# Queries normed head by head, softmax sums shared with VectorE, and more split tiles, in a fused decoder layer

## The chip, the cores and the metric

The kernel is written for one core of a Trainium2 chip. The metric is the device time of one execution in microseconds, taken as the median of several runs. The engines are TensorE (PE, with its weight loads PEld), VectorE (DVE), ScalarE (ACT), GpSimd (POOL) and SyncE (SP, which issues nearly all DMAs). Each works through its own queue in order and waits on semaphores.

## The reference

One decoder layer over `x` (4 batches, 256 rows, 512 features) and a context of 1601 rows per batch. Each of three parts ends in a residual and a layernorm:

```
self:   q, k, v = x Wq + bq, ...     attention over the 16 x 16 (d, e) pairs of each row
cross:  kv = [context; x]            1601 + 256 = 1857 keys
        q = rms_norm(x Wq) , k = rms_norm(kv Wk), v = kv Wv     32 heads of 128, 8 key heads
        out = softmax(q k^T / sqrt(128)) v Wo
route:  softmax over 64 logits, the 8 largest kept, out = x * sum + weights @ expert_bias
```

All is float32. The cross attention is nearly all of the work, and the change lies in it.

## The kernel before

**Units and tiles.** A unit is one batch with one key head; there are 32 (8 per batch), and v is a unit's number. Its four query heads times 256 rows make two half-units p of 512 columns, 64 in all. The 1857 keys are 15 tiles j of 128 rows (the last has 65). For each tile of each half-unit PE computes scores, keys on the partitions and queries on the 512 columns; ACT copies them out of PSUM with the key's norm as scale; DVE raises `running_max`. Eighteen steps (`WAIT`) later DVE subtracts the column maximum (`shift`, L1636), ACT takes the exponential, and two steps after that (`LAG`) PE multiplies with the values into `OT_ps`.

**Precision.** To keep fp32 accuracy with fp32r matmuls, operands are split into a high and a low part and three products are summed (`three`, L971 to L973). A probability tile can be treated in two ways. A split tile has its exponential taken twice by ACT (`P_hi` rounded, then the full one in place, L1322 and L1323), its low part by POOL (`P_lo`, L888), and three matmuls on PE. A full tile has one exponential, no low part, and one full-precision matmul (L1001, two records in the profile). `FULL` lists the full tiles j of each batch.

**Softmax sums.** POOL adds every tile of a half-unit into `acc` (L902, L906). At the end PE transposes `acc` in four pieces (job `AT`, L1134), DVE sums along the columns and takes the reciprocal, PE transposes that (job `RT`, L1140), DVE copies it to `rrow`, and two DMAs store it in memory and spread it to all partitions (`rinv_spread`). DVE then divides the output (`divide`, L1811), ACT rounds it (`OT_high`), and DVE forms its low part (`OT_low`, L1815) for the product with `Wo` (jobs `O`).

**Queries.** Two Q tiles of 128 rows with four heads each are computed per unit (jobs `Q`), copied by DVE to `natq`, and multiplied by the inverse norm of each row and head: `normalise`, one `tensor_tensor` of 128x512 per tile with the factor broadcast along 128 columns (L1675). POOL computes the factors (`newton`). PE transposes the result (jobs `QT`, L1111).

**Order.** All engines walk over the same steps s, and a table written by hand (`fill`) says which other jobs stand in a step, by c = (s + 20) mod 30. One unit is 30 steps. In the order of the table: `Q` at c = 1, 3, 7, 9; `AT` at 10 and 25; `RT` at 12 and 27; `QT` at 15 and 27; `O` at 11, 13, 21, 23; `KV` (keys and values of the next unit) at each even c. DVE drains a job one step later, before what else it has in the step; each of its steps begins with `shift` and `raise_max`. `raise_max` of step s has to be done before PE's scores of step s + 2. The factor for the queries is used at c = 13 of DVE; `QT` at c = 15 of PE waits for both tiles (`s_nat`). POOL's steps are `P_lo`, the sum, and sometimes the norms' Newton steps, a weight split (first batch only) or products of the self attention of later row tiles, which are spread over single steps (`EVENTS`).

Of the kernel before, what the change touches and what calls it, by code (L numbers as in the profile page):

```python
# [23 lines left out]
P = 128  # L24
# [21 lines left out]
def layer(nc, x_in, sWq, sbq, sWk, sbk, sWv, sbv, ctx_in, Wq, Wk, Wv, Wo, qw, kw, x1, y_out, Wr, rb, eb, final):  # L46
# [25 lines left out]
    FULL = [[2, 3, 6, 7, 10, 11, 14], [4, 5, 10, 11, 14], [6, 7, 14], [6, 7, 14]]  # L72
    FULL = [FULL[v // KVH] for v in range(UNITS)]
    HALF = [[j for j in range(NJ) if j not in FULL[v]] for v in range(UNITS)]
# [75 lines left out]
    def fill(s):  # L150
# [5 lines left out]
        if c % 2 == 0:  # L156
# [9 lines left out]
            12: [("RT", 2 * v - 3)],  # L166
# [9 lines left out]
            27: [("RT", 2 * v - 2), ("QT", v, 1)],  # L176
# [5 lines left out]
        def real(job):  # L182
            if job[0] == "X":
                return job[1] < B and job[2] < NJ
            if job[0] in ("FR", "FT", "FL", "FW", "FM"):
                return True
            return 0 <= job[1] < (HALVES if job[0] in ("RT", "O", "MT", "AT") else UNITS)
# [3 lines left out]
    def divided(s):  # L191
        return [x[1] for x in fill(s - 6) if x[0] == "RT"]
# [111 lines left out]
    def acc_no(s):  # L304
        p, j = divmod(s, NJ)
        return (NJ - 1) * p + j
# [4 lines left out]
    def left(kind, v, at):  # L311
        return NJ * (2 * v - 3) + max(kind[v - 2][at]) + 1 if kind[v - 2][at] else 0

    with ExitStack() as ctx:
# [86 lines left out]
        built = [sb(f"built{i}", [P, 2, C, P], F32R) for i in range(2)]  # L401
# [3 lines left out]
        sums = sb("sums", [P, 2, 4])  # L405
        rinv = sb("rinv", [P, 2, 4])
        rrow = sb("rrow", [4, P])
# [113 lines left out]
        s_ri = sem("row_reciprocal")  # L521
# [38 lines left out]
        def xrow_of(k):  # L560
            return row[0] if k < CTX and k % 2 else xrow[:]

# [35 lines left out]
        def _(e):  # L598
# [103 lines left out]
            def store_tile(b, n):  # L702
                k = x_no(b, n)
                src = tile[k % 3] if b == 0 else built[k % 2]
# [26 lines left out]
            def store_reciprocals(p):  # L731
                e.wait_ge(s_fr, F_AT["RT", p] + 1)
                e.dma_start(rsd[p % 2].rearrange("(i q) -> i q", q=P), rrow[:]).then_inc(s_rd, 16)
# [47 lines left out]
            for s in STEPS:  # L781
# [25 lines left out]
                for x in fill(s - 1):  # L807
                    if x[0] == "RT":
                        store_reciprocals(x[1])
                for x in fill(s - 3):  # L810
                    if x[0] == "RT":
# [30 lines left out]
        def _(e):  # L842
# [4 lines left out]
            for i in range(2):  # L847
                e.memset(f(built[i][:]), 0.0).then_inc(s_pad, 1)
                e.memset(nat[i][:], 0.0).then_inc(s_pad, 1)
            e.memset(eps[:], EPS).then_inc(s_pad, 1)  # L850
# [40 lines left out]
            def add(t):  # L891
                p, j = divmod(t, NJ)
                if j == 0:
# [4 lines left out]
                if j == 1:  # L898
                    if p >= 2:

                        e.wait_ge(s_ff, F_AT["AT", p - 2] + 1)
# [3 lines left out]
                e.wait_ge(s_acc, acc_no(t - 1))  # L905
# [60 lines left out]
        def _(e):  # L966
            e.wait_ge(s_id, 2)
            e.wait_ge(s_pad, 5)
# [919 lines left out]
```

## Time and profile before

| | us |
|---|---|
| median of 3 runs (2812.94 to 2818.02) | 2815.64 |
| the profiled execution | 2816.99 |
| its span in the profile | 2815.2 |

| engine | busy us | share of the span | instructions |
|---|---|---|---|
| PE | 2720.3 | 97% | 14812 |
| PEld | 2220.4 | 79% | 14812 |
| POOL | 2377.3 | 84% | 2320 |
| DVE | 2221.7 | 79% | 3596 |
| ACT | 2029.4 | 72% | 3945 |

A time stands for one execution; the span is from its first to its last profiled instruction. Matmuls are pipelined and their ends are modelled, so consecutive ones overlap in the records, and a price is better read from starts. Durations of DVE and POOL instructions contain the time that they wait for a port to memory.

### The profile page before, as it was taken

Reading aid. Unit: us, or ns where it says so; the run is one execution under the profiler, and the core shown is the slowest. Engines: PE = TensorE matmul, PEld = TensorE weight load, DVE = VectorE, ACT = ScalarE, POOL = GpSimd, SP = SyncE. Lnnn points to the kernel's source line nnn. Section 1 sums busy time; section 2 is a strip of 40 time slices with the busy share of each in tenths; the row PEclk is TensorE's granted clock in tenths of the full one; section 3 lists DMA queues with packets and bytes.
Section 4 is the critical chain, followed back from the end, with each engine's and each line's share of the span. In section 5 each row is a group of like instructions: output and inputs, shape, how many; then the busy total and the mean of one; then the engine's idle time right before and its main releaser. Section 6 shows DMA issues by size and latency. Waiting matters only on the chain.

```text
span 2815.2 us, 47816 instructions
## 1 busy us (share of the span) xinstructions
PE 2720.3 (97%) x14812; PEld 2220.4 (79%) x14812; DVE 2221.7 (79%) x3596; ACT 2029.4 (72%) x3945; POOL 2377.3 (84%) x2320
## 2 busy tenths in 40 slices
PE   7899999999999999999999999999999999999974
PEld 5777878777878888888888888888888888888853
DVE  5577888888778878888778887787778888788873
ACT  3577777777767777777777777777777777777771
POOL 4399999898888888878889988888898888888893
PEclk9999999999999999999999999999999999999996
DMA  6756565565555454555545455554455445344310
GB/s 234 253 184 216 193 221 193 195 213 184 183 178 200 160 177 169 182 177 196 178 147 193 167 189 174 179 184 165 156 173 173 154 158 180 124 165 150 117 42 26
DMA packets 159434, 485.64 MB, mean 173 GB/s; under 512 B 16839, under 2 KB 27849, under 8 KB 159182
## 3 DMA queue, kind: packets, MB, share of 16 engines
q1 hardware_dynamic: 157592, 481.01, 50.5%
q8 instruction: 121, 1.98, 0.3%
q10 hardware_dynamic: 1590, 1.58, 0.2%
q14 instruction: 131, 1.07, 0.1%
HBM read 403.09 MB, written 79.43 MB: 171 GB/s over the span
## 4 chain that ended last, share of the span: by engine, by line
PE 79%; POOL 9%; issue 6%; DVE 4%; ACT 2%; DMA 1%; SPq 0%; POOLq 0%; ACTq 0%; DVEq 0%
PE K_ps L971 9%; PE K_ps L973 9%; PE K_ps L972 9%; PE OT_ps L1001 7%; PE S_ps L971 6%; PE S_ps L973 6%; PE S_ps L972 6%; POOL acc L906 5%; PE OT_ps L971 5%; PE OT_ps L972 4%; PE OT_ps L973 4%; POOL P_lo L888 2%; PE F_ps L971 2%; PE F_ps L972 2%; PE F_ps L973 2%
## 5 line engine op out<-in xcount | busy, mean ns | idle before, releaser
L906 POOL TENSOR_TENSOR acc<-acc,scores 128x512 f32<-128x512 f32 (+1 forms) x832 | 1120.8, 1347 | 40.4 <-ACT scores L1323 10.1
L888 POOL TENSOR_TENSOR P_lo<-scores,P_hi 128x512 fp32r<-128x512 f32 x672 | 898.4, 1337 | 211.3 <-ACT scores L1323 210.3
L1652 DVE SCALAR_TENSOR_TENSOR running_max<-S_ps,rk,running_max 128x512 f32<-128x512 f32 (+1 forms) x896 | 669.0, 747 | 250.2 <-ACT scores L1309 247.8
L1636 DVE TENSOR_TENSOR scores<-scores,Mb_ps 128x512 f32<-128x512 f32 (+1 forms) x960 | 648.7, 676 | 134.4 <-PE Mb_ps L1127 134.3
L1309 ACT ACTIVATE scores<-S_ps,rk 128x512 f32<-128x512 f32 (+1 forms) x960 | 651.6, 679 | 139.8 <-PE S_ps L973 120.1
L1323 ACT ACTIVATE scores<-scores 128x512 f32<-128x512 f32 (+1 forms) x960 | 596.9, 622 | 59.2 <-DVE scores L1636 57.1
L1322 ACT ACTIVATE P_hi<-scores 128x512 fp32r<-128x512 f32 x672 | 423.1, 630 | 293.7 <-DVE scores L1636 213.9
L971 PE MATMUL S_ps<-QT_hi,KT_hi 128*128 128x512 f32 (+1 forms) x960 | 496.9, 518 | 14.8 <-DVE running_max L1652 13.0
L971 PE MATMUL K_ps<-Wkv_hi,kvT 128*128 128x256 f32 (+1 forms) x1664 | 470.9, 283 | 2.4 <-DVE kvT L1709 2.4
L973 PE MATMUL K_ps<-Wkv_hi,kvT 128*128 128x256 f32 (+1 forms) x1664 | 471.1, 283 | 0.0
L972 PE MATMUL K_ps<-Wkv_lo,kvT 128*128 128x256 f32 (+1 forms) x1664 | 470.3, 283 | 0.0
L973 PE MATMUL S_ps<-QT_hi,KT_lo 128*128 128x512 f32 (+1 forms) x960 | 380.6, 396 | 0.0
L972 PE MATMUL S_ps<-QT_lo,KT_hi 128*128 128x512 f32 (+1 forms) x960 | 379.3, 395 | 0.0
L971 PEld LDWEIGHTS K_ps<-Wkv_hi,kvT 128*128 128x128 f32 (+1 forms) x1664 | 310.3, 186 | 22.4 <-DVE kvT L1709 2.8
L972 PEld LDWEIGHTS K_ps<-Wkv_lo,kvT 128*128 128x128 f32 (+1 forms) x1664 | 310.3, 186 | 20.1
L971 PE MATMUL OT_ps<-P_hi,V_hi 128*128 128x512 f32 x672 | 290.3, 432 | 31.0 <-POOL P_lo L888 30.8
L973 PEld LDWEIGHTS K_ps<-Wkv_hi,kvT 128*128 128x128 f32 (+1 forms) x1664 | 310.7, 187 | 0.0
L1001 PE MATMUL OT_ps<-scores,V_full 128*128 128x512 f32 (+1 forms) x576 | 296.7, 597 | 0.0
L971 PEld LDWEIGHTS S_ps<-QT_hi,KT_hi 128*128 128x128 f32 (+1 forms) x960 | 178.1, 186 | 119.3 <-DVE running_max L1652 46.5
L972 PE MATMUL OT_ps<-P_lo,V_hi 128*128 128x512 f32 x672 | 266.6, 397 | 0.0
L973 PE MATMUL OT_ps<-P_hi,V_lo 128*128 128x512 f32 x672 | 266.0, 396 | 0.0
L972 PEld LDWEIGHTS S_ps<-QT_lo,KT_hi 128*128 128x128 f32 (+1 forms) x960 | 178.9, 186 | 92.4 <-issue 64.1
(226 smaller groups left out, 4666.8 us busy)
## 6 DMA issues: line engine op xcount, KB each, us to landing
kvT<-kvT_scratch SPq DMA_DIRECT2D x403, 512.0 KB, 3.7
Wq_hi<-weight_halves_scratch SPq DMA_DIRECT2D x48, 512.0 KB, 5.4
Wq_lo<-weight_halves_scratch SPq DMA_DIRECT2D x48, 512.0 KB, 6.6
Wo_hi<-weight_halves_scratch SPq DMA_DIRECT2D x48, 512.0 KB, 4.7
Wo_lo<-weight_halves_scratch SPq DMA_DIRECT2D x48, 512.0 KB, 5.6
kvT_scratch<-built SPq DMA_DIRECT2D x45, 512.0 KB, 4.3
rinv_spread<-rinv_scratch SPq DMA_DIRECT2D x64, 256.0 KB, 4.8
Wkv_hi<-weight_halves_scratch SPq DMA_DIRECT2D x24, 512.0 KB, 5.6
```

What stands on the lines that cost most here:

```text
L888: e.tensor_tensor(P_lo[n % PB][0:r, :], prob(t)[0:r, :], f(P_hi[n % PB][0:r, :]), ALU.subtract)\
L906: e.tensor_tensor(a[0:r, :], a[0:r, :], prob(t)[0:r, :], ALU.add).then_inc(s_acc, 1)
L971: e.matmul(out, l_hi, r_hi, start=first, stop=False)
L972: e.matmul(out, l_hi, r_lo, start=False, stop=False)
L973: return e.matmul(out, l_lo, r_hi, start=False, stop=last)
L1001: ins = e.matmul(OT_ps[:], V_full[v % 2][0:r, FULL[v].index(j), :], row[t % RING][0:r, :], start=first, stop=last)
L1309: e.activation(row[s % RING][0:r, :], S_ps[s % 2][0:r, :], ACT.Copy, scale=rk[0:r, v % 2, j:j + 1])\
L1322: e.activation(P_hi[n % PB][0:r, :], d, ACT.Exp)
L1323: e.activation(d, d, ACT.Exp).then_inc(s_p, 1)
L1636: e.tensor_tensor(d, d, Mb_ps[0:r, :], ALU.add).then_inc(s_d, 1)
L1652: e.scalar_tensor_tensor(a, src, k, a, ALU.mult, ALU.max).then_inc(s_top, 1)
```

## The change

Five things, all in the cross attention:

- `normalise` is called for one Q tile at a time, tile 0 at c = 13 and tile 1 at c = 14 of DVE, and does four `tensor_scalar` of 128x128 per tile, one for each head, with the factor as a per-partition scalar.
- Tiles 2, 7 and 11 of each half-unit are no longer added into `acc`. DVE sums each of them in blocks of 32x32 (`tensor_reduce` with `apply_transpose`, 128x512 to 128x16), one step after its shift. In the last unit (`LATE`) all 15 tiles go this way and nothing is added on POOL. At the end DVE reduces `acc` in the same way and adds up the blocks (`sum_blocks`, at c = 9 and 24).
- Job `AT` is now one product of 16x32 on PE, `sums` times a 0/1 matrix `same`, which gives the row sums in the layout of `rrow`; DVE takes the reciprocal straight into `rrow`. The four transposes of `acc`, the job `RT`, its copy and its reciprocal go.
- The store and the spread of the reciprocals follow `AT` and so come two steps earlier; `divide`, `OT_high` and `OT_low` come one step earlier.
- The lists of full tiles shrink from 7, 5, 3, 3 to 5, 3, 1, 1 tiles for the four batches. The products of the later self attention go to the steps of tiles 2, 7, 11 (`LIGHT`). `built` has one buffer in place of two.

```diff
-    FULL = [[2, 3, 6, 7, 10, 11, 14], [4, 5, 10, 11, 14], [6, 7, 14], [6, 7, 14]]
+    FULL = [[0, 1, 12, 13, 14], [12, 13, 14], [14], [14]]
+    SUMMED = [[2, 7, 11]] * B
+    LIGHT = [[2, 7, 11]] * B
+    SUMMED = [SUMMED[v // KVH] for v in range(UNITS - 1)] + [list(range(NJ))]
...
-            12: [("RT", 2 * v - 3)],
...
-            27: [("RT", 2 * v - 2), ("QT", v, 1)],
+            27: [("QT", v, 1)],
...
     def divided(s):
-        return [x[1] for x in fill(s - 6) if x[0] == "RT"]
+        return [x[1] for x in fill(s - 7) if x[0] == "AT"]
...
-        if j in FULL[p // 2] and j - 1 not in FULL[p // 2] and j < NJ - 1:
+        if j in LIGHT[p // 2]:
             EVENTS.append(s)
...
+            def add_blocks(p):
+                e.wait_ge(s_bt, p + 1)
                 out = take(("AT", p))
-                for i in range(4):
-                    ins = e.transpose(out[:, i * P:(i + 1) * P], acc[p % 2][:, i * P:(i + 1) * P], ident[:])
+                e.matmul(out[0:16, 0:32], sums[:, p % 2, :], same[:], start=True, stop=True).then_inc(s_ff, 1)
...
-            def normalise(v):
+            def normalise(v, t):
                 e.wait_ge(s_nw, 5 * RT_AT["q", v] + 5)
-                e.wait_ge(s_kr, K_AT["Q", v, 1] + 1)
-                for t in range(TPB):
-                    factor = rq[:, 4 * t:4 * t + 4].unsqueeze(2).to_broadcast([P, GR, HD])
-                    e.tensor_tensor(natq[t][:], natq[t][:], factor, ALU.mult).then_inc(s_nat, 1)
+                e.wait_ge(s_kr, K_AT["Q", v, t] + 1)
+                for h in range(GR):
+                    ins = e.tensor_scalar(natq[t][:, h, :], natq[t][:, h, :], rq[:, 4 * t + h:4 * t + h + 1], None, ALU.mult)
+                ins.then_inc(s_nat, 1)
...
-                    e.reduce_sum(sums[:, p % 2, :], out.rearrange("p (i k) -> p i k", k=P), AX.X).then_inc(s_fr, 1)
-                    e.reciprocal(rinv[:, p % 2, :], sums[:, p % 2, :]).then_inc(s_ri, 1)
+                    e.reciprocal(rrow[:], out[0:16, 0:32]).then_inc(s_fr, 1)
...
+            def sum_tile(t):
+                p, j = divmod(t, NJ)
+                e.wait_ge(s_p, t + 1)
+                e.tensor_reduce(blocks_of(p)[:, SUMMED[p // 2].index(j), :], prob(t).rearrange("p (j a) -> p j a", a=32), AX.X,
+                                ALU.add, apply_transpose=True).then_inc(s_bs, 1)
...
-                for kind, v in rooted(s - 4):
-                    if kind == "q":
-                        normalise(v)
+                for t in range(TPB):
+                    for kind, v in rooted(s - 4 - t):
+                        if kind == "q":
+                            normalise(v, t)
+                if 0 <= s - WAIT - 1 < NS and summed_tile(s - WAIT - 1):
+                    sum_tile(s - WAIT - 1)
+                for x in fill(s + 1):
+                    if x[0] == "AT":
+                        sum_blocks(x[1])
```

## Rows read from the trace of the kernel before

**Rows 1.** The page, busy time of each engine.
```profile
PE 2720.3 (97%) x14812; PEld 2220.4 (79%) x14812; DVE 2221.7 (79%) x3596; ACT 2029.4 (72%) x3945; POOL 2377.3 (84%) x2320
```

**Rows 2.** Stages: stretch, its us, busy PE, PEld, DVE, ACT, POOL, clock, DMA.
```profile
88.80:748.80 660.00, 646.24 (x3509) 522.25 (x3510) 524.71 (x846) 488.60 (x927) 576.39 (x543) 0.99 0.60 206
748.80:2062.80 1314.00, 1309.51 (x7295) 1087.68 (x7294) 1059.78 (x1690) 994.98 (x1946) 1148.36 (x1141) 1.00 0.52 176
2062.80:2651.00 588.20, 582.90 (x3252) 485.74 (x3251) 492.05 (x813) 439.27 (x868) 509.26 (x507) 1.00 0.46 152
...
2720.00:2815.20 95.20, 50.71 (x148) 30.44 (x146) 40.96 (x79) 23.66 (x45) 47.94 (x38) 0.71 0.10 34
```

**Rows 3.** Timeline of PE: start us, us, what it is.
```profile
1508.06 1.02 PE L1001 MATMUL OT_ps<-scores,V_full 65*128 65x512 f32 x2
...
1509.16 0.39 PE L972 MATMUL S_ps<-QT_lo,KT_hi 128*128 128x512 f32 x1
1509.39 0.40 PE L973 MATMUL S_ps<-QT_hi,KT_lo 128*128 128x512 f32 x1
1509.63 0.60 PE L1134 MATMUL F_ps<-ident,acc 128*128 128x128 f32 x4
1510.06 0.60 PE L1102 MATMUL F_ps<-ident,nat 128*128 128x128 f32 x4
```

**Rows 4.** Groups by line: count, busy us, mean ns, idle before.
```profile
L906 POOL TENSOR_TENSOR acc<-acc,scores 128x512 f32<-128x512 f32 x768 | 1038.4, 1352 | 31.2 <-ACT scores L1323 10.1 <-POOL acc L906 0.4
L888 POOL TENSOR_TENSOR P_lo<-scores,P_hi 128x512 fp32r<-128x512 f32 x672 | 898.4, 1337 | 211.3 <-ACT scores L1323 210.3
...
L1660 DVE TENSOR_REDUCE ss_k<-sq 128x4 f32<-128x512 f32 x96 | 65.3, 680 | 30.1 <-ACT sq L1419 29.9
...
L945 POOL TENSOR_TENSOR Wq_lo<-w_stage,Wq_hi 128x1024 fp32r<-128x1024 f32 x16 | 38.6, 2414 | 8.8 <-ACT Wq_hi L1449 8.8
```

**Rows 5.** DMA issues: what, count, KB, median us to landing.
```profile
kvT_scratch<-built SPq DMA_DIRECT2D x45, 512.0 KB, 4.3
```

**Rows 6.** Instructions of three lines: least, median, most ns.
```profile
L1675 DVE TENSOR_TENSOR natq<-natq,rq x64: 669/1764/2155, 83.7 to 2633.0; 128x512 f32<-128x512 f32 x64
...
L1776 DVE TENSOR_SCALAR w_stage<-w_stage,self_small x12: 534/547/1652, 2194.6 to 2661.3; 128x512 f32<-128x512 f32 x12
...
L1768 DVE TENSOR_SCALAR self_small<-self_small x8: 170/686/891, 2189.6 to 2809.7; 128x2 f32<-128x2 f32 x8
```

**Rows 7.** Timeline of DVE at a normalisation.
```profile
1802.63 3.34 DVE L1675 TENSOR_TENSOR natq<-natq,rq 128x512 f32<-128x512 f32 x2
1805.89 0.68 DVE L1636 TENSOR_TENSOR scores<-scores,Mb_ps 128x512 f32<-128x512 f32 x1
1806.49 0.74 DVE L1652 SCALAR_TENSOR_TENSOR running_max<-S_ps,rk,running_max 128x512 f32<-128x512 f32 x1
```

**Rows 8.** Timeline of POOL at the same place.
```profile
1802.43 1.29 POOL L888 TENSOR_TENSOR P_lo<-scores,P_hi 128x512 fp32r<-128x512 f32 x1
1803.68 1.74 POOL L906 TENSOR_TENSOR acc<-acc,scores 128x512 f32<-128x512 f32 x1
1805.38 1.75 POOL L888 TENSOR_TENSOR P_lo<-scores,P_hi 128x512 fp32r<-128x512 f32 x1
```

**Rows 9.** Timeline of ACT at the same place.
```profile
1803.46 0.62 ACT L1323 ACTIVATE scores<-scores 128x512 f32<-128x512 f32 x1
```

**Rows 10.** Timeline of PE at the same place.
```profile
1808.26 0.40 PE L971 MATMUL S_ps<-QT_hi,KT_hi 128*128 128x512 f32 x1
...
1808.95 0.60 PE L1111 MATMUL F_ps<-ident,natq 128*128 128x128 f32 x4
```

**Rows 11.** Timeline of POOL and DVE in the last half-unit.
```profile
2737.64 1.27 POOL L902 TENSOR_TENSOR acc<-scores 128x512 f32<-128x512 f32 x1
...
2765.83 2.68 POOL L906 TENSOR_TENSOR acc<-acc,scores 128x512 f32<-128x512 f32 x2
...
2780.74 0.69 DVE L1811 TENSOR_TENSOR OT_n<-OT_n,rinv_spread 128x512 f32<-128x512 f32 x1 [5.61 <-DMA rinv_spread<-rinv_scratch]
```

More of the change, by code:

```diff
@@ L312, in left @@
         return NJ * (2 * v - 3) + max(kind[v - 2][at]) + 1 if kind[v - 2][at] else 0
+    BLOCKS = []
+    for s in STEPS:
+        if 0 <= s - WAIT - 1 < NS and summed_tile(s - WAIT - 1):
+            BLOCKS.append(s - WAIT - 1)
+        BLOCKS += [("acc", x[1]) for x in fill(s + 1) if x[0] == "AT" and x[1] not in LATE]
+    BLOCK_AT = {x: n for n, x in enumerate(BLOCKS)}
     with ExitStack() as ctx:
@@ L400, in layer @@
         xrow = sb("xrow", [P, E])
-        built = [sb(f"built{i}", [P, 2, C, P], F32R) for i in range(2)]
+        built = sb("built", [P, 2, C, P], F32R)
         ident = sb("ident", [P, P])
@@ L404, in layer @@
         nm = sb("nm", [P, 2, 4])
-        sums = sb("sums", [P, 2, 4])
-        rinv = sb("rinv", [P, 2, 4])
-        rrow = sb("rrow", [4, P])
+        blocks = sb("block_sums", [P, 2, max(map(len, SUMMED[:-1])) + 1, 16])
+        sums = sb("block_totals", [P, 2, 16])
+        same = sb("same_in_block", [P, 32])
+        rrow = sb("rrow", [16, 32])
         rb_all = sb("rinv_spread", [P, QW])
@@ L703, in store_tile @@
                 k = x_no(b, n)
-                src = tile[k % 3] if b == 0 else built[k % 2]
+                src = tile[k % 3] if b == 0 else built
                 e.wait_ge(s_fr, F_AT["X", b, n] + 1)
@@ L847, in _ @@
             for i in range(2):
[L848 removed]
                 e.memset(nat[i][:], 0.0).then_inc(s_pad, 1)
+            e.memset(f(built[:]), 0.0).then_inc(s_pad, 1)
             e.memset(eps[:], EPS).then_inc(s_pad, 1)
@@ L892, in add @@
                 p, j = divmod(t, NJ)
-                if j == 0:
+                if t not in ADD_AT:
                     return
@@ L1307, in copy_scores @@
                         e.wait_ge(s_pv, t + 1)
-                    e.wait_ge(s_acc, acc_no(t + 1 if t % NJ == 0 else t))
+                    if summed_tile(t):
+                        e.wait_ge(s_bs, BLOCK_AT[t] + 1)
+                    else:
+                        e.wait_ge(s_acc, ADD_AT[t + 1 if t % NJ == 0 else t] + 1)
+                if r < P and p in LATE:
+                    e.activation(row[s % RING][TAIL // 32 * 32:P, :], row[s % RING][TAIL // 32 * 32:P, :], ACT.Copy,
+                                 scale=0.0).then_inc(s_z, 1)
+                    e.wait_ge(s_z, LATE.index(p) + 1)
                 e.activation(row[s % RING][0:r, :], S_ps[s % 2][0:r, :], ACT.Copy, scale=rk[0:r, v % 2, j:j + 1])\
@@ L1706, in drain @@
                         k = x_no(b, n)
-                        to = tile[k % 3] if b == 0 else built[k % 2]
+                        to = tile[k % 3] if b == 0 else built
                         hi, dst = to[:, 0, :, 0:r], to[:, 1, :, 0:r]
```

81 lines of the change are left out of this document (49 added, 32 removed).

## The prediction

> **What bounds the kernel now.** I read the busy shares first: TensorE is busy 97% of the span [rows 1]. Then the stages: between 749 and 2063 us PE is busy 1309.5 of 1314 us, at full clock, while DVE, ACT and GpSimd (POOL) each have room [rows 2]. In the first batch PE idles 13.8 of 660 us, and only after 2720 us is it really idle, 44.5 of 95 us [rows 2]. So for some 2560 us the order of work on PE sets the time, and another engine counts only when it makes PE wait. After 2720 us it is the other way round: POOL runs a low part and a sum for each tile without a pause, and PE has time to spare [rows 11].
>
> A busy PE is not PE at its peak, so PE prices are taken from starts. A 512-column fp32r matmul starts 0.23 us after the one before (1509.16 to 1509.39). A full-precision PV tile takes from 1508.06 to 1508.93, 0.87 us (the next score's second matmul, at 1509.16, is 0.23 behind its first). A split tile is three times 0.23, 0.69 us [rows 3].
>
> **What PE gets back.** Each half-unit drops four transposes of `acc`, 0.43 us (1509.63 to 1510.06 [rows 3]), and one transpose of the reciprocals, a quarter of that, 0.11. It adds one product with 32 columns. No row has one; a 512-column full tile is two passes of 0.43, so 32 columns are at least 2 x 0.03 us; two passes at the price of a 128-column transpose are at most 0.22; I take 0.1, nearer to the narrow end. 0.44 us x 62 half-units = 27 us (the last two belong to the tail).
> The four batches' lists of full tiles hold 7, 5, 3 and 3 tiles before and 5, 3, 1 and 1 after, each for 16 half-units: 288 become 160, and 128 tiles become split, four in each unit. 124 of them lie outside the tail: x 0.18 us = 22 us. PE's saving is 49 us (bounds 42 to 53) if nobody else becomes late.
>
> **What the others do.** POOL loses the sums of tiles 2, 7 and 11 in 62 half-units and all 28 of the last two, 214 x 1.35 = 288 us, and gains 128 low parts x 1.34 = 171 us [rows 4]: 117 us less. DVE gains 216 block sums and 62 reductions of `acc`. The nearest row is a plain 128x512 reduction, 0.68 us [rows 4]; the transposed form has none. It reads the same columns, so I put nothing below that; above I allow twice, 1.36; I take 0.68, the row's. 278 x 0.68 = 189 us, less 64 x 0.68 = 44 for the reduction of the transposed sums that goes; the small reciprocals, copies and totals about cancel. DVE has 254 us idle between 749 and 2063 us alone [rows 2], and nothing waits on a block sum within its step: 0, or +25 us if it costs double and meets two drains in a step. The total of an `acc` is needed by PE one step later: 0, or 0.3 us x 62 = 19 where the scores' drains come first. ACT gets 128 more exponentials of 0.62 us [rows 9] and 32 copies; it idles 319 of those 1314 us [rows 2]: 0. The single `built` buffer needs its store landed (4.3 us [rows 5]) before the next build, six steps of 2.7 us later at the closest: 0. The division and its low part move one step earlier, and the DMAs of the reciprocals two; the spread has four steps to land where it had three: 0. In the first batch POOL's weight splits (2.4 us [rows 4]) now fall on steps that also have a low part (tiles 3, 7, 11), so POOL runs behind there by about 1.2 us a unit: 0 to 10 us, and 0 where PE is late anyway for the next reason.
>
> **The normalisation of the queries.** This is where I expect the loss. Before, DVE does two instructions of 128x512. The least of the 64 is 0.67 us, the median 1.76 [rows 6]: most of it is waiting, and the timeline shows for what. The pair starts at 1802.63 [rows 7] under POOL's low part of 1802.43, which ends at 1803.72; the second of the pair sits under POOL's sum of 1803.68, which itself lasts 1.74 instead of 1.29 us, because it let the first DVE instruction pass [rows 8]. The two engines take turns, whole instruction by whole instruction: 3.34 us for 1.3 us of work. Of the 32 pairs, for which this one stands, 29 have a second instruction of over 1.5 us: POOL got in between.
> The change makes eight instructions of 128x128 of the two, four in each of two steps, single-source with a scalar. Do these take turns too? A 128x512 one takes 0.53 us alone and up to 1.65, and one of 128x2 takes 0.17 alone and 0.69 in the median [rows 6]. So size doesn't protect: the price is per instruction, 0.26 us each (between 0.17 for 2 columns and 0.54 for 512), plus the rest of a POOL instruction whenever POOL has one ready.
> The Trainium skill has a rule for this: the GPSIMD Engine Reference (8. Key points) says that POOL shares its SBUF interfaces with VectorE and contends with DVE instructions in a two-port mode or with two SBUF inputs, and VectorE: DVE Perf Modes (The perf-mode tier table) gives fp32 `tensor_scalar` from SBUF the doubled rate that uses both ports. By that rule the new form is quicker alone and no freer of POOL than the old; the trace agrees, by the 0.69 us of the two-column instruction.
>
> Now the steps, by the clock of rows 7 to 10. At 1802.5 POOL has four instructions to hand: low part and sum of one tile, and of the next, whose exponential ends at 1804.08 [rows 9]. None is saved by the change (the tiles there are 4 and 5, and 6 in the step after). POOL instructions are 1.25 us apart, about 1.35 with a short DVE one let through; they end at 1803.7, 1805.05, 1806.4 and 1807.75, and one DVE instruction goes after each. The first four are done at 1808.0, where the whole pair had been done at 1805.97. The next shift and maximum take 0.6 and 0.75, to 1809.35; PE's next scores, planned for 1808.26 [rows 10], come 1.1 us late. The drain of the output goes on to 1809.9. Tile 6's exponentials, begun when its shift ends at 1808.7, end at 1809.85, so POOL again has two instructions ready: the second four end at 1809.9 + 2 x 1.3 + 0.7 = 1813.2. The transposes of the queries, planned for 1808.95 [rows 10], wait for the eighth: **4.3 us late**, the 1.1 included. Before, the pair had ended 3 us ahead of them. DVE and POOL catch up while PE stands still, so I see no second stall behind it.
> That is 4.3 us in each of 31 units, times 29/32 for the share of pairs in which POOL came between: 121 us. Bounds: if POOL never gets in between, the first four take 1.2 + 4 x 0.26 = 2.3 us, the second four no more, and all end before 1808.95: 0. If in the first batch a weight split of 2.4 us lies ahead of the first instruction, 1 us more in 7 units: 128.
>
> **The tail.** In the last half POOL's tiles take from 2737.64 to 2768.51, 30.9 us for 15, at two instructions each [rows 11]. Without the sums one is left; POOL (1.3 us), DVE (shift and block sum, 2 x 0.6 by starts) and ACT (two exponentials of 0.6) are then about level: 15 x 1.3 = 19.5 us, 11 less. In the half before, PE still has scores, and I take 8. Between the last sum and the division at 2780.74 [rows 11] lie four transposes, a reduction and a second transposition beside the two DMAs; a small reduction and a product take their place, for which I take 3 us off. 22 us in all (bounds 8 and 30).
>
> **Sum.** PE idles 23.6 us between 89 and 2651 us [rows 2]; a third of that should fall into the new waits, -8. So -27 - 22 - 22 + 121 - 8 = +42 on the profiled execution's 2816.99 us (span 2815.2), 2859 us. That execution was 1.35 above the median 2815.64; against the median 2858.
>
> **Rivals.**
> - A, not slower: POOL doesn't get in between the four short instructions, or once only. For it: in 3 of 32 pairs it didn't, and four in a row offer themselves within 1 us. Against: the other 29, and a short instruction holds the port for less of its time than a long one, which leaves POOL more room. It decides below two POOL instructions per four. 2816.99 - 71 = 2746, against the median 2745; with POOL behind in the first batch up to 2755.
> - B: POOL comes between about half the time. The first four end near 1806, the second near 1810.5, 1.5 us late: 47 - 71 = -24, against the median 2792 us.
> - C: the transposed reduction costs double. 25 us on top of the forecast, 2883.
> - D: the tail doesn't give its 22 us, since DVE with its block sums becomes what it waits for: 2880.
>
> **Chances.** The forecast's case, C and D in it, 0.60 (2825 to 2890 alone); A 0.28; B 0.12. A measurement here can tell 0.2% (5.6 us) from no change. Slower: the 0.60 and 0.01 of B; within: 0.04 of B; faster: A and the other 0.07, 0.35. The range 2742 to 2890 holds A, B and nearly all of the forecast's case.
>
> **What would show it.** Right: the DVE timeline at the normalisation has groups of four short instructions that last about 5 us, with a POOL instruction between each; the query transposes follow a PE gap of some 4 us per unit that is put down to `natq`; PE's idle time between 749 and 2063 us grows from 4.5 to some 60. PE's own saving is right if its busy time falls by about 45 us all the same; POOL's by about 117; the tail's if the last half's tiles come 1.3 us apart. Wrong: short instructions with a median near 0.26 us, a PE as full as now and a time near 2746; or a transposed reduction far over 0.68 us.

## The result, and the profile after

The changed kernel takes 2958.11 us (median of 4 runs, 2953.44 to 2963.43) against 2816.83 for the kernel before beside it: ratio 1.0502, 95% interval 1.0484 to 1.052, **141 us slower**. The forecast was 42 us slower, 2858, in a range of 2742 to 2890. Its direction came out, and so did the mechanism of its largest term; its sum was 99 us short.

The page of the kernel after, busy times (span 2961.6 us), against [rows 1]:

```profile
PE 2758.3 (93%) x14748; PEld 2253.4 (76%) x14748; DVE 2524.2 (85%) x4003; ACT 2088.7 (71%) x4107; POOL 2245.0 (76%) x2233
```

POOL lost 132 us (forecast 117) and DVE gained 302. The stages, columns as in [rows 2], from the first scores on; the last is the tail:

```profile
93.30:780.00 686.70, 642.64 (x3399) 518.39 (x3400) 588.05 (x907) 484.79 (x933) 536.42 (x512) 0.96 0.57 191
780.00:2180.00 1400.00, 1338.40 (x7303) 1113.44 (x7302) 1218.18 (x1898) 1030.32 (x2038) 1105.64 (x1115) 0.98 0.50 168
2180.00:2816.80 636.80, 604.77 (x3296) 501.23 (x3295) 558.55 (x913) 462.28 (x924) 493.18 (x503) 0.97 0.43 142
2885.20:2961.60 76.40, 42.69 (x142) 27.02 (x142) 49.17 (x98) 26.68 (x51) 23.59 (x18) 0.77 0.13 42
```

PE idled 4.5 of 1314 us before [rows 2]; now it idles 61.6 of 1400 ("some 60" was the sign given). Two other signs did not show: PE's busy time should have fallen by 45 us and rose by 38, since many matmuls now run at half clock (in e1 below, without the short instructions, it falls by 16); and the low parts of the last half come 1.5 us apart (14 in 21.0 us), not 1.3. The waits of PE name the reason (us in total, times, the longest):

```profile
PE F_ps L1132 <- DVE natq L1699: 75.6, 31, 2.7
PE S_ps L992 <- DVE running_max L1677: 49.4, 53, 3.1
PE OT_ps L992 <- POOL P_lo L909: 18.5, 28, 1.8
PE F_ps L1139 <- DVE running_max L1677: 12.4, 17, 3.2
```

One wait in each unit but the first: the transposes of the queries wait for the last normed tile. The groups behind it, against [rows 4, 6]:

```profile
L1699 DVE TENSOR_SCALAR natq<-natq,rq 128x128 f32<-128x128 f32 x256 | 250.8, 1038 | 1.0 <-POOL rq L951 0.3
L1831 DVE TRANSPOSE_TENSOR_REDUCE block_sums<-scores 128x16 f32<-128x512 f32 x186 | 128.9, 693 | 0.0
...
L1841 DVE TRANSPOSE_TENSOR_REDUCE block_sums<-acc 128x16 f32<-128x512 f32 x62 | 43.5, 702 | 0.5 <-POOL acc L927 0.4
```

A normalising instruction of 128 columns takes 1038 ns in the mean, and 270 at least; the transposed reduction costs 0.69 us, as taken (so not rival C).

**Read one unit closely.** DVE of the kernel after in unit 21 (start us, us, what), to lay beside [rows 7]:

```profile
1912.70 0.75 DVE L1677 SCALAR_TENSOR_TENSOR running_max<-S_ps,rk,running_max 128x512 f32<-128x512 f32 x1 [0.39 <-ACT scores L1330]
1913.44 5.05 DVE L1699 TENSOR_SCALAR natq<-natq,rq 128x128 f32<-128x128 f32 x4
1918.41 0.67 DVE L1661 TENSOR_TENSOR scores<-scores,Mb_ps 128x512 f32<-128x512 f32 x1
1919.01 0.74 DVE L1677 SCALAR_TENSOR_TENSOR running_max<-S_ps,rk,running_max 128x512 f32<-128x512 f32 x1
1919.67 0.67 DVE L1773 TENSOR_TENSOR y<-y,F_ps 128x512 f32<-128x512 f32 x1
1920.26 2.90 DVE L1699 TENSOR_SCALAR natq<-natq,rq 128x128 f32<-128x128 f32 x4
```

POOL at the same place:

```profile
1913.36 1.29 POOL L909 TENSOR_TENSOR P_lo<-scores,P_hi 128x512 fp32r<-128x512 f32 x1
1914.61 1.30 POOL L927 TENSOR_TENSOR acc<-acc,scores 128x512 f32<-128x512 f32 x1
1915.85 1.31 POOL L909 TENSOR_TENSOR P_lo<-scores,P_hi 128x512 fp32r<-128x512 f32 x1
1917.10 1.30 POOL L927 TENSOR_TENSOR acc<-acc,scores 128x512 f32<-128x512 f32 x1
1920.34 1.32 POOL L909 TENSOR_TENSOR P_lo<-scores,P_hi 128x512 fp32r<-128x512 f32 x1 [1.94 <-ACT scores L1344]
1921.62 1.26 POOL L927 TENSOR_TENSOR acc<-acc,scores 128x512 f32<-128x512 f32 x1
```

Count: the first four short instructions last 5.05 us beside four POOL instructions, each short one until a POOL instruction ends; the second four last 2.90 beside two (their own durations are 0.27, 1.29, 1.30 and 0.27 us). Without POOL four last 0.86 (unit 0). PE there:

```profile
1919.80 0.50 PE L992 MATMUL S_ps<-QT_hi,KT_hi 128*128 128x512 f32 x1 [0.55 <-DVE running_max L1677]
...
1923.22 0.93 PE L1132 MATMUL F_ps<-ident,natq 128*128 128x128 f32 x4 [2.47 <-DVE natq L1699]
1923.80 0.78 PE L992 MATMUL OT_ps<-P_hi,V_hi 128*128 128x512 f32 x1
1924.37 0.63 PE L993 MATMUL OT_ps<-P_lo,V_hi 128*128 128x512 f32 x1
1924.80 0.63 PE L994 MATMUL OT_ps<-P_hi,V_lo 128*128 128x512 f32 x1
```

PE waits 0.55 and 2.47 us, and then its 512-column matmuls start 0.43 us apart (1924.37 to 1924.80), not 0.23 [rows 3]. The windows say why (columns as in [rows 2]; the granted clock is the value behind POOL's):

```profile
1920.00:1923.20 3.20, 0.75 (x3) 0.28 (x2) 3.20 (x6) 1.90 (x5) 2.54 (x2) 1.00 0.97 338
1923.20:1926.60 3.40, 3.38 (x11) 2.81 (x12) 3.40 (x7) 2.81 (x6) 1.29 (x1) 0.54 0.34 134
```

After 3.2 us with PE busy for 0.75, 3.4 us are granted 0.54, about the lower level (1.2 GHz). Between the first and the last scores the trace has 33 such stretches at half clock, 157 us in all, at least one in nearly every unit; the kernel before has 3 there, 10 us.

### The profile page after: what moved, and what is told of

Same layout as the page of the kernel before. It is cut to its first block, busy times and chain, and to the rows that moved or that the text cites. A ratio compares the mean times of both kernels' runs of the same rounds, so it can differ in the third digit from the quotient of the medians.

```text
span 2961.6 us, 48211 instructions
## 1 busy us (share of the span) xinstructions
PE 2758.3 (93%) x14748; PEld 2253.4 (76%) x14748; DVE 2524.2 (85%) x4003; ACT 2088.7 (71%) x4107; POOL 2245.0 (76%) x2233
## 4 chain that ended last, share of the span: by engine, by line
PE 56%; POOL 15%; DVE 13%; issue 12%; ACT 2%; DMA 1%; POOLq 0%; ACTq 0%; SPq 0%; DVEq 0%
DVE natq L1699 7%; PE K_ps L992 6%; PE K_ps L993 6%; PE K_ps L994 6%; POOL acc L927 6%; POOL P_lo L909 5%; PE S_ps L992 5%; PE S_ps L994 4%; PE S_ps L993 4%; PE OT_ps L992 4%; PE OT_ps L994 4%; PE OT_ps L993 4%; PE OT_ps L1022 3%; DVE running_max L1677 2%; DVE scores L1661 1%
## 5 line engine op out<-in xcount | busy, mean ns | idle before, releaser
L909 POOL TENSOR_TENSOR P_lo<-scores,P_hi 128x512 fp32r<-128x512 f32 x800 | 1055.1, 1320 | 451.3 <-ACT scores L1344 450.6
L1343 ACT ACTIVATE P_hi<-scores 128x512 fp32r<-128x512 f32 x800 | 504.1, 630 | 499.2 <-DVE scores L1661 348.8
L927 POOL TENSOR_TENSOR acc<-acc,scores 128x512 f32<-128x512 f32 x620 | 829.3, 1338 | 33.0 <-ACT scores L1344 23.2
L992 PE MATMUL S_ps<-QT_hi,KT_hi 128*128 128x512 f32 (+1 forms) x960 | 448.7, 467 | 52.0 <-DVE running_max L1677 49.4
L992 PE MATMUL K_ps<-Wkv_hi,kvT 128*128 128x256 f32 (+1 forms) x1664 | 478.5, 288 | 2.4 <-DVE kvT L1734 2.4
L994 PE MATMUL K_ps<-Wkv_hi,kvT 128*128 128x256 f32 (+1 forms) x1664 | 475.9, 286 | 0.0
L992 PE MATMUL OT_ps<-P_hi,V_hi 128*128 128x512 f32 x800 | 351.0, 439 | 19.1 <-POOL P_lo L909 18.5
L992 PEld LDWEIGHTS K_ps<-Wkv_hi,kvT 128*128 128x128 f32 (+1 forms) x1664 | 319.5, 192 | 24.1 <-DVE kvT L1734 2.9
L993 PE MATMUL OT_ps<-P_lo,V_hi 128*128 128x512 f32 x800 | 321.4, 402 | 0.0
L994 PE MATMUL OT_ps<-P_hi,V_lo 128*128 128x512 f32 x800 | 320.8, 401 | 0.0
L994 PEld LDWEIGHTS K_ps<-Wkv_hi,kvT 128*128 128x128 f32 (+1 forms) x1664 | 317.9, 191 | 0.0
L1699 DVE TENSOR_SCALAR natq<-natq,rq 128x128 f32<-128x128 f32 x256 | 250.8, 1038 | 1.0 <-POOL rq L951 0.3
```

What stands on the lines that cost most here:

```text
L909: e.tensor_tensor(P_lo[n % PB][0:r, :], prob(t)[0:r, :], f(P_hi[n % PB][0:r, :]), ALU.subtract)\
L927: e.tensor_tensor(a[0:r, :], a[0:r, :], prob(t)[0:r, :], ALU.add).then_inc(s_acc, 1)
L992: e.matmul(out, l_hi, r_hi, start=first, stop=False)
L993: e.matmul(out, l_hi, r_lo, start=False, stop=False)
L994: return e.matmul(out, l_lo, r_hi, start=False, stop=last)
L1343: e.activation(P_hi[n % PB][0:r, :], d, ACT.Exp)
```

## The experiments

Times are medians; ratios are against the kernel before, run beside them. Its median was 2815.5 to 2818.9 us on the different occasions, so a difference between two of these times is good to about 3 us. "Unit" is one head's cycle of 30 score tiles, measured between first score matmuls; c is the step in it. Each experiment has a name (e1, e2, ...) that is used later.

**1. Take the change apart.** e1 is the changed kernel with the normalisation of before (both tiles in one step):

```diff
-            def normalise(v, t):
+            def normalise(v):
...
-                for h in range(GR):
-                    ins = e.tensor_scalar(natq[t][:, h, :], natq[t][:, h, :], rq[:, 4 * t + h:4 * t + h + 1], None, ALU.mult)
-                ins.then_inc(s_nat, 1)
...
+                for t in range(TPB):
+                    factor = rq[:, 4 * t:4 * t + 4].unsqueeze(2).to_broadcast([P, GR, HD])
+                    e.tensor_tensor(natq[t][:], natq[t][:], factor, ALU.mult).then_inc(s_nat, 1)
```

> The changed kernel with only the normalisation of before (two 128x512 instructions at c = 13). Theory 1 (turn-taking of the eight short DVE instructions with POOL, and what PE loses after the stall): all of the loss is gone and the saving of the rest shows, 2816.8 - 71 = 2746, between 2738 and 2765. Rival (DVE is overloaded by the block sums, the normalisation only adds to it): over 2850.

e1 measured 2833.16, ratio 1.0059 (1.0044 to 1.0074), which neither theory had. So the normalisation costs 125 us in the changed kernel, near the 121 of the forecast, and all the rest costs 16 us where a saving of 71 had been forecast: 87 us are missing there. e2 is the kernel before with only the new normalisation:

> The kernel before with only the new normalisation (eight 128x128 instructions, four each at c = 13 and 14). Theory 1: the trace of the changed kernel shows units 5.4 us longer than their PE work in the middle batches and 7 to 9 in the others, so 31 x 5.4 to 31 x 7: 2816.8 + 167 to 217, 2985 to 3030; about 5 us a unit at least, over 2960. Rival (overload by the block sums): 2816.8 + 31 x 1 to 2, 2850 to 2880.

e2 measured 2899.58, ratio 1.0298 (1.0279 to 1.0316), between the two theories: alone the normalisation costs 83. It costs 42 more beside the other parts of the change, so the parts don't simply add up.

**2. The clock.** e5: 22 transposes whose result nobody reads, on PE, ahead of the wait for the normed queries.

> The changed kernel with 22 transposes of the identity (0.11 us each, 2.4 us, results overwritten) put on PE just before it waits for the normed queries, as long as its gap there (2.47 us). Theory of the clock: PE's clock falls to half for 3.4 us after each such gap, 1.7 us lost a unit; with PE busy through the wait the clock stays up: 31 x 1.7 = 53 us less, 2905. Rival (what is lost beyond the gap is DVE and POOL catching up): no change, 2950 to 2970.

2946.43, ratio 1.0454 (1.0436 to 1.0472). The mean granted clock of the profiled executions rises from 0.966 to 0.985, as high as in e1, but the time falls by 12 us only (53 was the theory): the wait is DVE's and stays. By units: 17 to 22 fall from 85.3 to 84.2 us, 23 to 30 from 88.9 to 87.4, but units 1 to 14 gain nothing. There PE gets steps c = 15 and 16 faster and then waits longer in the steps behind. So the half clock costs some 1.1 to 1.5 us a unit where DVE and POOL have no other backlog, and is hidden behind their backlog elsewhere.

**3. The normalisation on ACT** (e6), eight `activation(..., scale=rq)`, out of POOL's way:

> The changed kernel with the eight 128x128 normalisations on ACT (activation with the factor as scale) instead of DVE. Theory 1: ACT shares no port with POOL, so each lasts about 0.3 us as its 128x128 instruction in the trace (0.31), no waiting: as fast as the old form or a little faster, since DVE is free of 3.2 us a unit: 2735 to 2750. Rival: ACT is late with its exponentials at c = 13 and 14, 1 us each: over 2770.

2834.57, ratio 1.0074 (1.0051 to 1.0098), the same as the old form on DVE and not the 2735 to 2750 of theory 1. The 256 short ones last 387 to 423 ns on ACT, beside the same POOL, and PE waits for them once. So eight short instructions cost nothing on an engine that doesn't take turns with POOL; what was still missing lay elsewhere.

**4. Where the other 87 us are.** All start from e1 (2833 us). The lines that differ from e1 (for e8 to e10 only the new one is shown):

```diff
 e7  -        return [x[1] for x in fill(s - 7) if x[0] == "AT"]
     +        return [x[1] for x in fill(s - 8) if x[0] == "AT"]
 e8  +    SUMMED = [[]] * B
 e9  +    FULL = [[2, 3, 6, 7, 10, 11, 14], [4, 5, 10, 11, 14], [6, 7, 14], [6, 7, 14]]
 e10 +    LIGHT = [[2, 6, 10]] * B
```

> After with the normalisation of before (2833 us), and the division and the low parts that follow it put back into the steps of before (steps 18 and 3 of the cycle, not 17 and 2). The first version's whole loss against its expectation (about 88 us) is unexplained. Theory 1, VectorE's step 17 is overfull (in units 1 to 7 it took 3.8 us there against 2.1 before, then ScalarE's and TensorE's steps 18 wait): about 20 us come back, 2808 to 2818. Rival, the place of the division does not matter, only the work added to VectorE does: 2828 to 2838.

e7: 2834.08, ratio 1.0061 (1.0046 to 1.0076): the division's place costs nothing here; theory 1 fell.

> After with the normalisation of before (2833 us), and GpSimd adding the tiles 2, 7 and 11 of each half again, except in the last unit: only the accumulated tile is reduced by blocks. Theory 1, VectorE's block sums (six a unit of 0.69 us, 129 us in all) delay the score copies' readers while it is the fuller engine: 2785 to 2805. Rival, GpSimd was the late engine in the first batch, and what VectorE took from it was paid back: 2830 to 2850.

e8: 2891.14, ratio 1.0267 (1.0251 to 1.0283), **58 us slower** than e1, the opposite of theory 1 and more than the rival's: the block sums are the best part of the change. Units 1 to 7 take 92.0 us each instead of 87.5.

> After with the normalisation of before (2833 us), and the list of unsplit tiles of before. The prediction priced the 124 more split tiles at 22 us of TensorE: by that 2855. Rival, the further splits cost on the other engines (low parts on GpSimd, high parts on ScalarE) what they save on TensorE in the first half of the run: 2825 to 2840.

e9: 2804.75, ratio 0.9954 (0.9939 to 0.997), **28 us faster** than e1, more than the rival's 8 at most: with the old list of unsplit tiles it beats the kernel before by half a per cent. The further splits lose where they should have gained 22. By units: unit 0 +4.2 us for the changed list, units 1 to 7 +2.8 each, 8 to 14 +0.5, but 17 to 22 -0.35. Look at unit 4 of e1, DVE and then POOL:

```profile
504.55 0.70 DVE L1831 TRANSPOSE_TENSOR_REDUCE block_sums<-scores 128x16 f32<-128x512 f32 x1
505.17 2.69 DVE L1622 TENSOR_TENSOR self_x<-self_x,self_small 128x512 f32<-128x512 f32 x1
507.79 0.67 DVE L1661 TENSOR_TENSOR scores<-scores,Mb_ps 128x512 f32<-128x512 f32 x1
```

```profile
503.67 1.32 POOL L909 TENSOR_TENSOR P_lo<-scores,P_hi 128x512 fp32r<-128x512 f32 x1
504.92 2.39 POOL L966 TENSOR_TENSOR Wo_lo<-w_stage,Wo_hi 128x1024 fp32r<-128x1024 f32 x1
507.26 1.74 POOL L909 TENSOR_TENSOR P_lo<-scores,P_hi 128x512 fp32r<-128x512 f32 x1
```

POOL had no gap since tiles 10 and 11 became split: its weight split starts late and sits in front of the two-source `self_x`, which waits to its end. The next scores come 2.9 us late. With the old list POOL had idled 2.0 us before that weight split and PE waits 0.6 there. In units 1 to 6 PE waits 16.3 us for `running_max` against 5.1.

> After with the normalisation of before (2833 us), and the later self-attention products issued beside tiles 2, 6 and 10 (the places of the first batch before) in place of 2, 7 and 11; all else as there. With 2, 7 and 11 their VectorE sums, three steps on, fall into steps 17 and 2, where the moved division stands too; with 2, 6 and 10 they fall into 16 and 1. Theory 1 (that meeting makes step 17 late): 2808 to 2820. Rival: 2828 to 2838.

e10: 2852.17, ratio 1.0125 (1.0104 to 1.0146), 19 slower than e1: theory 1 fell again, and the rival missed too. Beside 6 and 10 POOL now has a low part and a sum; beside 7 and 11 DVE had taken the sum. That suggests that the number of instructions that POOL has in one step counts; e14 and e19 below put this to the test, with mixed success.

**5. The same parts with the old list of unsplit tiles.** e11 has the new normalisation:

> The changed kernel with nothing but the list of unsplit tiles put back. The same edit took 28 us off the version with the old normalisation (2833 to 2805). The new normalisation cost 125 us in the changed kernel and 83 us in the kernel before. Theory 1, the extra 42 us come from GpSimd, which the splits made late in the first batches: here it costs 83, 2883 to 2895. Rival, they come from VectorE's block sums, which leave it no time to catch up after the eight short instructions: 2920 to 2935.

2880.31, ratio 1.0219 (1.0193 to 1.0244): against e9 the normalisation costs 76, although the block sums are there, so the extra comes from the splits. The trace shows it directly; DVE, POOL and PE in unit 21, to lay beside the fences above:

```profile
1852.93 5.05 DVE L1699 TENSOR_SCALAR natq<-natq,rq 128x128 f32<-128x128 f32 x4
...
1859.75 1.53 DVE L1699 TENSOR_SCALAR natq<-natq,rq 128x128 f32<-128x128 f32 x4
```

```profile
1859.32 1.29 POOL L927 TENSOR_TENSOR acc<-acc,scores 128x512 f32<-128x512 f32 x1 [1.42 <-ACT scores L1344]
```

```profile
1861.34 0.66 PE L1132 MATMUL F_ps<-ident,natq 128*128 128x128 f32 x4 [1.07 <-DVE natq L1699]
```

Tile 6 is unsplit, POOL has one instruction there and not two, the second four last 1.53 us and not 2.90, PE waits 1.07 and not 2.47, and no half-clock stretch follows. In units 10 to 16, where tiles 4 and 5 are unsplit, the first four last 2.93. So the splits make the wait 1.4 us longer, and behind the longer wait comes the half clock.

> The version with the old normalisation and the old list of unsplit tiles (2805 us), with GpSimd adding tiles 2, 7 and 11 again outside the last unit: before's division of labour, save for the reduction of the accumulated tile, the tail and the places of the self-attention products. With the longer list of splits this edit cost 58 us. Theory 1, GpSimd is late only where it has the splits' low parts as well: 2795 to 2808 here. Rival, it is late in the first batch in either case, because products now meet additions at 7 and 11: 2815 to 2840.

e15: 2825.44, ratio 1.0027 (1.0017 to 1.0037), in the rival's range: here the block sums give 21 us (58 with the splits).

> The version with the old normalisation, the old list of unsplit tiles and no block sums outside the last unit (2825 us), with the later self-attention products beside the tiles of before (2, 6, 10 in batch 0; 4, 10 in batch 1; 6 in the others). It differs from the kernel before by the block reduction of the accumulated tile with its one product, the division one step earlier, the single buffer for built tiles, and the last unit. Theory 1, three products a half in batch 1 beside split tiles cost there (units 8 to 14 took 84.7 us each against 83.0): 2800 to 2812. Rival, the places are worth nothing outside the split list: 2820 to 2828.

e18: 2814.23, ratio 0.9992 (0.9983 to 1.0002), between the two theories: the places of the products were worth 11 us, most of it in batch 0 (units 1 to 7 fall from 85.2 to 84.4 us) and not in batch 1, where theory 1 had put it (84.7 to 84.3). The rest of the change (block reduction of `acc` and one product, earlier division, one buffer, last unit) is no gain that can be told from none.

> The version with the old normalisation and the old list of unsplit tiles (2805 us), with the last unit handled as all others: GpSimd adds all its tiles but 2, 7 and 11, VectorE reduces the sum at the end. The prediction gave the tail 22 us: by that 2824 to 2829. Rival D of the prediction, that the tail gives nothing: 2803 to 2808.

e13: 2809.76, ratio 0.9975 (0.9965 to 0.9985), against 2804.75 in e9: putting all sums of the last unit on DVE gives 5 us net. It takes 8.4 off the stretch from the last scores to the end (85.8 to 77.4), and costs 5.0 in unit 31 itself (63.6 to 68.6).

> The version with the old normalisation and the old list of unsplit tiles (2805 us), with VectorE's block sums put on tiles for which GpSimd also has a low part (4, 8, 12 in batch 0; 2, 7, 12 in batch 1; none in batches 2 and 3), and the self-attention products beside tiles 2, 6 and 10, which have no low part in batch 0. Theory 1, what counts is GpSimd's load step by step: 2788 to 2800. Rival, VectorE's load counts and the places are worth nothing: 2803 to 2812.

e14: 2811.58, ratio 0.998 (0.997 to 0.9989), 7 slower than e9 and in the rival's range. Batch 0 got faster (83.8 us a unit against 84.7), batches 1 and 3 slower (84.6 against 83.7, and 85.3 against 84.8 in units 25 to 30). So theory 1 held in batch 0 alone. Since sums and products moved together, the run doesn't say which of them slowed batch 1.

**6. The normalisation's price, from both sides.** e3: the short instructions joined, the two steps kept:

```diff
-                for h in range(GR):
-                    ins = e.tensor_scalar(natq[t][:, h, :], natq[t][:, h, :], rq[:, 4 * t + h:4 * t + h + 1], None, ALU.mult)
-                ins.then_inc(s_nat, 1)
+                factor = rq[:, 4 * t:4 * t + 4].unsqueeze(2).to_broadcast([P, GR, HD])
+                e.tensor_tensor(natq[t][:], natq[t][:], factor, ALU.mult).then_inc(s_nat, 1)
```

> The changed kernel with each of the two normalising steps doing its tile by one broadcast multiplication over 512 columns (as before the change) in place of four of 128; steps, waits and all else as in the changed kernel (2958 us). Theory 1, the price lies in the eight short instructions taking turns with GpSimd (5.05 and 2.90 us for the two tiles in units 15 to 31): two of about 1.8 us leave the second tile at most 1.1 us shorter but the first 3.2 us, the wait at step 15 goes, and 2840 to 2865. Rival, the price lies in giving the second tile its own later step: 2900 to 2930.

2832.62, ratio 1.0055 (1.0036 to 1.0075), the time of e1: the later step costs nothing, **cutting each multiplication in four costs all 125 us**. The edit changes the kind of instruction too, but alone the two kinds differ little (0.86 us for four of 128 columns, 0.68 for one of 512). The other side, e17: eight short ones with unsplit tiles around them,

```diff
-    FULL = [[0, 1, 12, 13, 14], [12, 13, 14], [14], [14]]
+    FULL = [[2, 3, 4, 5, 6, 7, 14], [4, 5, 6, 7, 14], [4, 5, 6, 7, 14], [4, 5, 6, 7, 14]]
```

> The changed kernel with the unsplit tiles put where the queries are normalised (2 to 7 and 14 in batch 0, 4 to 7 and 14 in the other batches), so that GpSimd has one operation a step there, not two. That is two more unsplit tiles in each half of batches 2 and 3 than before the change, about 0.16 us each. Theory 1, how long the eight short instructions take is set by what GpSimd has queued beside them: in the version with the old list they took 2.93 us for the first tile where tiles 4 and 5 were unsplit and 1.53 for the second where 6 and 7 were; here they take both, and the normalisation's cost falls from 76 us there (2880) to under 20: 2820 to 2850. Rival, the splits slow the changed kernel through GpSimd's total, not at this place: 2875 to 2895.

2821.26, ratio 1.0018 (1.0008 to 1.0028), as theory 1 had it, **137 us under the changed kernel** by one list. Its DVE and POOL:

```profile
1737.21 2.93 DVE L1699 TENSOR_SCALAR natq<-natq,rq 128x128 f32<-128x128 f32 x4 [0.39 <-POOL rq L951]
...
1741.92 1.52 DVE L1699 TENSOR_SCALAR natq<-natq,rq 128x128 f32<-128x128 f32 x4
```

```profile
1737.13 2.73 POOL L927 TENSOR_TENSOR acc<-acc,scores 128x512 f32<-128x512 f32 x2
1741.48 1.28 POOL L927 TENSOR_TENSOR acc<-acc,scores 128x512 f32<-128x512 f32 x1 [1.62 <-ACT scores L1344]
```

The missing corner, e21, has the same list with the old form:

> The changed kernel with the normalisation of before and the unsplit tiles at 2 to 7 and 14 in batch 0, 4 to 7 and 14 in the others: the partner of the kernel with the new normalisation and this list (2821 us). Theory 1, the short instructions cost little where GpSimd has one operation a step beside them: 2805 to 2815, that is 6 to 16 us for the normalisation against 125 with the changed list. Rival, this list is simply faster for all, the normalisation costs 75 still: about 2746.

2804.38, ratio 0.9949 (0.9934 to 0.9964): the normalisation costs 17 us there (19 by the ratios). The four pairs:

| unsplit tiles | old form | new form | price |
|---|---|---|---|
| 4 to 7 (and 2, 3) | 2804.4 (e21) | 2821.3 (e17) | 17 |
| as before, changed kernel | 2804.8 (e9) | 2880.3 (e11) | 76 |
| as before, kernel before | 2816.8 | 2899.6 (e2) | 83 |
| as changed | 2833.2 (e1) | 2958.1 | 125 |

**7. Use it.** e19: old list, block sums on split tiles in batch 0 and the products on its unsplit ones (only the new lines):

```diff
+    SUMMED = [[4, 8, 12], [2, 7, 12], [2, 7, 11], [2, 7, 11]]
+    LIGHT = [[2, 6, 10], [4, 10], [6], [6]]
```

> The version with the old normalisation and the old list of unsplit tiles (2805 us), with block sums on 4, 8, 12 in batch 0, on 2, 7, 12 in batch 1, on 2, 7, 11 in batches 2 and 3, and the later self-attention products where they were before the change. Theory 1, GpSimd's load step by step sets batches 0 and 1 and VectorE's does not: 2788 to 2799. Rival: 2802 to 2812.

2801.14, ratio 0.9947 (0.9932 to 0.9962), 4 us under e9 and between the two theories. Then e20: batch 1's sums back on 2, 7, 11 and, from unit 16 on, one multiplication a tile in two steps:

> The combination (2801 us) with block sums on 2, 7, 11 in batch 1 too, and the normalisation as one broadcast multiplication a tile, in two steps from unit 16 on. Theory 1: units 17 to 30 get about 0.3 us each (as the one-operation form against the old one in the changed kernel, 80.24 against 80.58 us a unit), batch 1 about 0.2 each: 2793 to 2799. Rival, what is left in these units is TensorE's own work: 2800 to 2804.

**2791.77, ratio 0.991 (0.9893 to 0.9926)**, faster than both kernels. The reason given holds in part: units 8 to 14 gained 0.6 us each and 23 to 30 gained 0.4, but 17 to 22, with the same new form, gained nothing (80.9 against 81.0).

## Why the prediction was right and where it failed

The whole way in measured steps, beside what the prediction had for them:

| step | us | measured | forecast |
|---|---|---|---|
| before to e18 (reciprocals' path, division, tail) | 2816.8 to 2814.2 | -3, not told from 0 | -49 |
| products to tiles 2, 7, 11 (e15) | to 2825.4 | +11 | 0 |
| block sums of three tiles on DVE (e9) | to 2804.8 | -21 | 0 |
| changed list of unsplit tiles (e1) | to 2833.2 | +28 | -22 |
| short normalising instructions (the changed kernel) | to 2958.1 | +125 | +121, less 8 |

Two steps of the prediction failed, and they make up the 99 us: the split tiles (50) and the first row of the table (46). The other rows nearly cancel.

- **The normalisation** is right in its mechanism, turn-taking with POOL, and its size came out partly by luck. The first four were forecast at 5.5 us and lasted 5.05, the scores 1.1 late and came 0.55 late; the second four at 3.3, and lasted 2.90. The 4.3 us a unit came as 4.0 in the mean (125 / 31) and as 4.7 in units 17 to 22 (85.3 against 80.6 in e1). But it is made up otherwise: PE waits 3.0 us in unit 21, not 4.3, and most of the rest is lost at half clock, a term that the prediction hadn't. Step c = 16, which has no wait, takes 3.66 us against 2.84 in e11, where the wait is short; e5 brought 1.4 us back in c = 15 and 16 together.
- **The split tiles** are the step that failed most, by 50 us: -22 was forecast, +28 measured. TensorE's own price was right: at the three steps around tiles 6 and 7 a unit gains 0.33 us, twice, for four tiles (0.16 each; 0.18 forecast), and 0.3 goes again to a wait of `MT` (the job that transposes the maxima, at c = 5 and 20). The failure is "if nobody else becomes late": each split gives POOL 1.3 us in a given step. The prediction summed POOL over the run (117 us less) and wrote "0 to 10 us" for the steps where weight splits meet low parts; in batch 0 alone (units 0 to 7) they cost 24. The fences under e9 above show one such place.
- **The reciprocals' path on PE**: -27 was -15. Units 17 to 22, with nothing else late, fell from 81.40 us before to 80.93 in e9: 0.47 a unit, not 0.88. The product was put at 0.1 us, and at 0.22 at most. The kernel after shows it, and the last line is the same PV matmul in the kernel before:

```profile
1083.51 0.39 PE L994 MATMUL S_ps<-QT_hi,KT_lo 128*128 128x512 f32 x1
1083.82 0.23 PE L1156 MATMUL F_ps<-same_in_block,block_totals 128*16 128x32 f32 x2
1083.98 0.66 PE L1123 MATMUL F_ps<-ident,nat 128*128 128x128 f32 x4
1084.40 0.48 PE L992 MATMUL OT_ps<-P_hi,V_hi 128*128 128x512 f32 x1
```

```profile
1510.42 0.48 PE L971 MATMUL OT_ps<-P_hi,V_hi 128*128 128x512 f32 x1
```

  From the scores' third matmul to the PV matmul it is now 0.89 us (1083.51 to 1084.40), and 1.03 before (1509.39 [rows 3] to 1510.42). Four transposes of 0.43 us are gone and only 0.14 is gained, so the product costs 0.29. It had been priced by its 32 columns.
- **"The division and its low part move one step earlier ...: 0"** is the other term that failed. From 2816.8 us, -15 on the path and a tail shorter by 16 should have given -31 in e18; -3 was measured. PE's waits for the `MT` job, before and then in e18 (us in total, times, the longest):

```profile
PE F_ps L1118 <- DVE running_max L1652: 1.9, 3, 0.9
```

```profile
PE F_ps L1139 <- DVE running_max L1677: 23.5, 25, 3.2
```

  In e18 the low part `OT_lo` stands on DVE in front of the last `running_max` of a half, for which `MT` waits; in the kernel before it stood behind it (`running_max` at 1082.53, `OT_lo` at 1083.79). DVE and PE of e18 in unit 12:

```profile
1084.94 0.89 DVE L1857 TENSOR_TENSOR OT_lo<-OT_n,OT_hi 128x512 fp32r<-128x512 f32 x1
...
1087.78 0.74 DVE L1677 SCALAR_TENSOR_TENSOR running_max<-S_ps,rk,running_max 65x512 f32<-65x512 f32 x1
```

```profile
1088.57 0.66 PE L1139 MATMUL F_ps<-ident,running_max 128*128 128x128 f32 x4 [1.25 <-DVE running_max L1677]
```

  These waits grew by 22 us of the 28 that are missing (those for low parts fell by 12 at the same time). That the earlier low part is their cause is read from such places, not tested: no run put it back in e18, and in e7, with the changed list, putting it back halved the `MT` waits (13.8 to 7.3 us) but gained nothing.
- **Block sums on DVE** were put at 0 and give 21 us (58 with the changed list). The reason given for 0 (DVE has room) held; that POOL's three instructions fewer a half are worth something in batches 0 and 1 wasn't asked, since [rows 2] shows PE nearly full there. That PE was full because POOL just kept up fits these runs, but is argued.
- **The tail** held in size: from the last scores to the end 95.1 before, 76.4 after, -19 (22 forecast). But the shares are others. Putting all sums of the last unit on DVE, beyond the three of the other units, gives 5 net (e13), and the way from POOL's last instruction to the division is 5 us shorter (12.2 to 7.1), where 3 was forecast.
- **What stays open.** Of the `acc` reduction, the single buffer and the earlier division none was taken back alone from e18, so the rest of its 28 us has no cause shown; the largest part stands in units 8 to 14, which take 84.3 us against 83.0 before. Nor was it shown why block sums in batch 3 save 0.3 us a unit, and which places the sums and the products should have (e14, e19).

Rival A fell (POOL comes between all four), B and C too. Rival D was half right in its reason: in e13 against e9 DVE's sums do cost 5 us in unit 31.

## What to carry to other kernels

Where two engines take turns by whole instructions, the count of instructions makes the price: here 512 columns in one instruction waited once, and four of 128 waited up to four times. Price a step by what the other engine has queued in that same step, not by its sum over the run: POOL had 132 us less to do in all, and was late in single steps. When one engine is 97% busy, ask which other engine just keeps up with it before giving that one work. And when an item moves one step earlier, look which wait it now stands in front of.

## What the runs showed of the hardware

- Not all DVE instructions take turns with POOL. In the changed kernel the 186 transposed reductions of `scores` took 685 to 704 ns, beside POOL or not, and the scores' shift and maximum, which read PSUM, at most 0.69 and 0.76 us. The single-source multiplications of 128 columns in SBUF went from 270 ns to 2422, and the division with two SBUF sources from 649 to 4393:

```profile
L1831 DVE TRANSPOSE_TENSOR_REDUCE block_sums<-scores x186: 685/694/704, 143.5 to 2856.2; 128x16 f32<-128x512 f32 x186
```

  The Trainium skill says, in SBUF — State Buffer (Who interferes with whom), that whoever issues first holds the shared pair for its whole instruction, and that this concerns DVE's two-port modes and two SBUF inputs. The trace agrees with both parts: of the DVE instructions in the changed kernel only those that read and write SBUF alone grew, by up to the length of a POOL instruction or more (270 to 2422 ns above), while reductions and those with an operand in PSUM did not (685 to 704 ns above).
- On ACT the same multiplication of 128 columns took 387 to 423 ns in all 256 cases, beside the same POOL (e6).
- In unit 21 a wait of 2.47 us on TensorE was followed by 3.4 us at 0.54 of the clock; one of 1.07 us in e11 was not.
- One fp32 product of 32 columns between larger matmuls cost PE 0.29 us, as much as two thirds of four 128-column transposes (0.43).
- A multiplication by a factor per row took 1.77 us as one instruction of 512 columns beside POOL (e3, 0.68 alone), and 5.05 as four of 128 (0.86 alone).
